# A selective scan in one Macaron block: two 512-column scans per state in place of four 256-column ones

## The chip, the core and the metric

The kernel runs on one core of a Trainium2 chip. Its time is the device time of one launch in microseconds (us). Three runs of the kernel before gave 807.47, 808.60 and 809.86 us, so the median is 808.6 us.

A core has engines that each work through their own list of instructions in order: PE (matrix products), DVE (elementwise and scans), ACT (functions of one input, with a scale and a bias), POOL (elementwise, and here also the issue of adding DMAs) and SP (plain DMAs). They meet at semaphores only. An instruction that waits holds up everything behind it on its engine.

## The reference

```python
def _L0_attn_ref(x, W_x, W_dt, b_dt, A_log, D_param):          # d_inner 512, 16 states
    xz = einsum('bld,kd->blk', x, W_x)                         # dt_raw (128), b (16), c (16)
    dt = softplus(einsum('blr,dr->bld', dt_raw, W_dt) + b_dt)
    a = -exp(A_log)
    d_a = exp(dt[..., None] * a)                               # the decays
    dbx = dt[..., None] * b[:, :, None, :] * x[..., None]
    def step(h, (da_t, dbx_t, c_t)):
        h = da_t * h + dbx_t                                   # the scan over 2048 tokens
        return h, einsum('bdn,bn->bd', h, c_t)
    return scan(step, 0, ...) + x * D_param

x = x + 0.5 * ffn(layernorm(x), w1, w2, w3)      # ffn: w3q @ (sigmoid(w1q @ x) * (w2q @ x))
x = x + attn(layernorm(x), ...)                  # 2048 tokens x 512 channels
x = x + 0.5 * ffn(layernorm(x), w1, w2, w3)      # the same weights, quantised to -1, 0, 1
```

## The kernel before, in words

Channels lie on the partitions: 512 channels are four k-tiles of 128 (KD = 4). Tokens lie along the free axis in eight chunks of 256 (TC = 256, NC = 8). The scan stage goes through the chunks in order, and in each through the 16 states; one state of one chunk is a slot, number g = 16c + n. For a slot:

- POOL makes `dbx` for all four k-tiles in one instruction (`times_b`, L1146), two slots ahead of DVE, into a ring of four buffers.
- ACT makes the decays, one `Exp` of 128x256 for each k-tile, into two PSUM banks: `decay0` holds k-tiles 0 and 1, `decay1` holds 2 and 3 (`decays`, L747). A bank is free when its two scans of the slot before are done.
- DVE scans (`scans`, L941): four `tensor_tensor_scan` of 128x256, k-tile by k-tile, each started from the state that the same n had at the end of the chunk before (`last_state`; in chunk 0 from zero, as an immediate). Then it multiplies the states by the row c (`times_c`, L952, 128x1024) and keeps the last column (`save_state`, L957).
- POOL issues an adding DMA for the product (`add_prod`, L1159), even and odd states into two sums, and once a chunk adds the two sums (`add_y`, L1164).

Between these go the two FFNs and three layernorms (0, 1, 2: ahead of the first FFN, of the scan and of the second FFN) of neighbouring chunks. An FFN of a chunk is 11 ups (16 matmuls each) and 4 downs (22 each) on PE; for each up ACT takes `tanh` (L702), DVE the product `hid` (L907), ACT and POOL split it into `hid_hi` (L710) and `hid_lo` (L1126). DVE adds the downs to the sum (`residual`, L914). A layernorm goes PE mean, DVE `centred` (L887), ACT `square` (L669), POOL fold (L301, L303), PE variance, ACT `std` (L687), DVE reciprocal (L891), PE spread, DVE normalise (L895; its output is `xln` for layernorm 1). Softplus (L735), `Sqrt` and the set with `Exp` and `Tanh` are different tables on ACT, so that a change between them is an ACT_TABLE_LOAD.

Where these pieces stand between the scans is fixed by four tables, AT_PE, AT_ACT, AT_DVE and AT_POOL. A number 10s + p means slot s of the chunk, place p: on DVE place 0 is ahead of the first pair of scans, 1 between the pairs, 2 behind the second pair, 3 behind `save_state`; on ACT place 0 is ahead of the decays of pair 0 for slot s + 1, 1 between them and those of pair 1, 2 behind them. Names with `_first` and `_last` hold for the first and the last chunk. PE's numbers set only the order of its own pieces.

## Time and profile before

| | us |
|---|---|
| median of three runs | 808.6 |
| profiled execution | 809.69 |
| its span, first to last instruction | 807.9 |
| scan stage, first to last scan | 88.1 to 756.3 |
| a chunk in the steady part, from chunk to chunk | 88.8 |

Only the span has a trace; 1.8 us lie around it. Busy time of an engine is the union of its instructions in the trace. Successive instructions of one engine overlap a little, so that the distance from start to start (called pitch here) is less than the duration of one. In a timeline row the first number is the start, the second how long the row lasts, and x4 says that four like instructions stand in it; what stands in brackets is the idle time ahead of it and what ended that.

### The profile page before, as it was taken

What the parts mean: (1) busy time and instruction counts of PE and PEld (TensorE: products, weight loads), DVE (VectorE), ACT (ScalarE), POOL (GpSimd) and SP (SyncE); (2) the same over time, 40 slices, a digit from 0 to 9 for tenths busy, and PEclk for the clock granted to TensorE, in tenths of its full rate; (3) what the DMA queues carried; (4) which work ended last, traced back from release to release, by engine and by line L of the source; (5) the groups of instructions that cost most, each with busy time, mean ns of one, the idle gap of its engine ahead of it and who ended that gap; (6) DMA issues with size and microseconds to landing.
All of it is one profiled execution on the core that took longest, in us unless ns stands there. A gap on an engine that the chain in (4) does not pass through costs nothing.

```text
span 807.9 us, 13722 instructions
## 1 busy us (share of the span) xinstructions
PE 638.8 (79%) x4826; PEld 520.5 (64%) x4826; DVE 669.8 (83%) x1076; ACT 510.2 (63%) x1105; POOL 637.9 (79%) x522
## 2 busy tenths in 40 slices
PE   4598884398879979898789887997989878267788
PEld 4486763177568866777578666876677757155677
DVE  3962699799968999699979996899969997999721
ACT  5663755867685767567785768576756776556231
POOL 0442799989988999889998998799988989789011
PEclk9998997689999999999999999999999999778879
DMA  9400578886866688395958586669839585986300
GB/s 357 155 2 1 153 161 184 195 190 137 186 158 143 145 191 201 79 232 122 214 113 202 138 187 157 148 140 203 190 79 233 121 191 124 217 177 124 69 1 27
DMA packets 42725, 122.10 MB, mean 151 GB/s; under 512 B 5920, under 2 KB 14880, under 8 KB 42656
## 3 DMA queue, kind: packets, MB, share of 16 engines
q0 software_dynamic: 19152, 69.74, 44.8%
q1 hardware_dynamic: 23504, 51.49, 20.4%
q8 instruction: 38, 0.62, 0.3%
q14 instruction: 31, 0.25, 0.1%
HBM read 47.03 MB, written 4.46 MB: 64 GB/s over the span
## 4 chain that ended last, share of the span: by engine, by line
DVE 35%; PE 27%; POOL 14%; issue 14%; ACT 8%; DMA 3%; DVEq 1%; POOLq 0%; ACTq 0%
DVE states L941 20%; PE work L406 17%; DVE shared L952 8%; PE stat L406 7%; POOL shared L1146 5%; POOL hid_lo L1126 4%; POOL shared L1159 3%; DMA shared<-shared 2%; PE decay L406 2%; ACT decay L747 2%; DVE centred L887 1%; DVE hid L907 1%; DVE q L985 1%; ACT q L765 1%; ACT L687 1%
## 5 line engine op out<-in xcount | busy, mean ns | idle before, releaser
L406 PE MATMUL work<-x_hi,q 128*128 128x256 f16 x1408 | 329.1, 282 | 37.6 <-DVE hid L907 17.5
L1146 POOL TENSOR_TENSOR shared<-u,b_row 128x1024 f32<-128x1024 f32 x127 | 335.7, 2648 | 0.1
L406 PE MATMUL work<-x_lo,q 128*128 128x256 f16 x1408 | 328.6, 282 | 0.0
L941 DVE TENSOR_TENSOR_SCAN states<-decay,last_state,shared 128x256 f32<-128x256 f32 x448 | 301.7, 737 | 3.9 <-issue 0.6
L747 ACT ACTIVATE decay<-dt,a_neg 128x256 f32<-128x256 f32 x512 | 220.6, 467 | 99.9 <-DVE states L941 98.6
L406 PEld LDWEIGHTS work<-x_hi,q 128*128 128x128 f16 x1408 | 143.0, 102 | 68.9 <-DVE hid L907 25.0
L1126 POOL TENSOR_TENSOR hid_lo<-hid,hid_hi 128x256 f16<-128x256 f32 x176 | 132.5, 964 | 63.7 <-ACT hid_hi L710 63.6
L406 PE MATMUL work<-hid_hi,q 128*128 128x256 f16 x693 | 154.0, 273 | 11.9 <-POOL hid_lo L1126 8.0
L952 DVE TENSOR_TENSOR shared<-states,c_row 128x1024 f32<-128x1024 f32 x128 | 155.9, 1218 | 8.9 <-issue 0.2
L406 PEld LDWEIGHTS work<-x_lo,q 128*128 128x128 f16 x1408 | 142.2, 101 | 21.3
L406 PE MATMUL work<-hid_lo,q 128*128 128x256 f16 x693 | 153.8, 272 | 0.0
L1159 POOL DMA_DIRECT2D shared<-shared x126 | 130.7, 1038 | 26.5 <-DVE shared L952 18.5
L702 ACT ACTIVATE tanh<-work 128x256 f32<-128x256 f32 x176 | 62.4, 373 | 75.5 <-PE work L406 70.6
L907 DVE SCALAR_TENSOR_TENSOR hid<-tanh,work 128x256 f32<-128x256 f32 x176 | 71.0, 410 | 46.1 <-ACT tanh L702 44.7
L406 PEld LDWEIGHTS work<-hid_hi,q 128*128 128x128 f16 x693 | 68.4, 99 | 27.7 <-issue 12.8
L710 ACT ACTIVATE hid_hi<-hid 128x256 f16<-128x256 f32 x176 | 67.9, 409 | 13.7 <-DVE hid L907 13.3
L406 PEld LDWEIGHTS work<-hid_lo,q 128*128 128x128 f16 x693 | 67.8, 98 | 7.6
L1120 POOL TENSOR_TENSOR x_lo<-centred,x_hi 128x1024 f16<-128x1024 f32 x15 | 35.9, 2391 | 35.8 <-ACT x_hi L695 35.8
L406 PE MATMUL stat<-shared,mean_w 128*128 128x256 f32 x136 | 36.2, 414 | 24.8 <-DVE shared L914 11.8
L406 PEld LDWEIGHTS stat<-shared,mean_w 128*128 128x128 f32 x136 | 26.7, 207 | 31.3 <-DVE shared L914 14.1
L941 DVE TENSOR_TENSOR_SCAN states<-decay,shared 128x256 f32<-128x256 f32 x64 | 39.3, 679 | 3.2 <-ACT decay L747 2.3
L301 POOL TENSOR_TENSOR square<-square 128x512 f32<-128x512 f32 x21 | 34.6, 1650 | 7.9 <-ACT square L669 7.9
(100 smaller groups left out, 599.0 us busy)
## 6 DMA issues: line engine op xcount, KB each, us to landing
shared<-shared POOLq DMA_DIRECT2D x133, 512.0 KB, 6.3
b_row<-bc_dram SPq DMA_DIRECT2D x32, 512.0 KB, 4.9
c_row<-bc_dram SPq DMA_DIRECT2D x32, 512.0 KB, 5.3
x_in<-xT SPq DMA_DIRECT2D x8, 512.0 KB, 9.8
outT<-shared SPq DMA_DIRECT2D x7, 512.0 KB, 3.2
shared<-w1T SPq DMA_DIRECT2D x4, 704.0 KB, 7.7
shared<-w2T SPq DMA_DIRECT2D x4, 704.0 KB, 12.0
shared<-w3T SPq DMA_DIRECT2D x3, 768.0 KB, 13.4
```

Of the source, the lines that this page charges most:

```text
L301: engine.tensor_tensor(dst[:, 0:2, :], src[:, 0:2, :], src[:, 2:4, :], ALU.add).then_inc(summed, 1)
L406: return nc.tensor.matmul(out, lhsT, rhs, start=start, stop=stop)
L702: nc.scalar.activation(tanh[:, h % 3, :], bank_of(which, h)[:, 0, :], ACT.Tanh, scale=0.5 / X_SCALE).then_inc(tanh_done, 1)
L710: nc.scalar.activation(hid_hi[:, h, :], hid[:, hid_slot(which, h), :], ACT.Copy).then_inc(hi_done, 1)
L747: ins = nc.scalar.activation(decay[pair][:, j, :], dt[:, par, k, :], ACT.Exp, scale=a_neg[:, k, n:n + 1])
L907: nc.vector.scalar_tensor_tensor(out=hid[:, hid_slot(which, h), :], in0=tanh[:, h % 3, :], scalar=1.0, in1=bank_of(which, h)[:, 1, :], op0 ...
L941: nc.vector.tensor_tensor_scan(out=states[:, k, :], data0=decay[pair][:, k % 2, :], data1=dbx[:, g % DBX_RING, k, :], initial=state, op0=A ...
L952: nc.vector.tensor_tensor(prod_of(c, n), states[:, :, :], bcast(c_row[:, group % 2, n % ROWS, :]), ALU.mult).then_inc(prod_done, 1)
L1120: nc.gpsimd.tensor_tensor(x_lo[:, which, :, :], centred[i][:, :, :], x_hi[:, which, :, :], ALU.subtract).then_inc(ln_lo[i], 1)
L1126: nc.gpsimd.tensor_tensor(hid_lo[:, h, :], hid[:, hid_slot(which, h), :], hid_hi[:, h, :], ALU.subtract).then_inc(lo_done, 1)
L1146: nc.gpsimd.tensor_tensor(dbx[:, g % DBX_RING, :, :], u[:, par, :, :], bcast(b_row[:, group % 2, n % ROWS, :]), ALU.mult).then_inc(dbx_don ...
L1159: nc.gpsimd.dma_start(total, prod_of(c, n), accum_op=ALU.add).then_inc(added(c, n)[0], 16)
```

## The change

Each pair of scans becomes one scan of 128x512 over both k-tiles of the pair. For that the decay of the pair's second k-tile is zero in its first column, which cuts the recurrence there. DVE zeroes that column of both banks once, ahead of the scan stage, and the `Exp` of the second k-tile then writes columns 1 to 255 only. The state that the second k-tile should have started from enters through the input: `dbx[:, k, 0] += first_decay * last_state`. ACT does this (`add_carry`), one `Identity` of 128x1 for each pair with the carried state as input, the first decay as a scale read from memory and the old `dbx` as a bias read from memory. The first decays of a chunk (16 states each) are two more `Exp` of 128x16 a chunk (`first_decays`). In chunk 0 there is no carry.

New waits: the scan of a pair waits for its carry; `add_carry` waits for the slot's `dbx`, for the saved state of the chunk before and for the first decays. All four tables have new numbers.

```diff
 AT_ACT  (of 20 rows)
-    hi2=[100, 110, 122, 131, 131, 140, 140, 141, 142, 150, 150],
+    hi2=[82, 112, 112, 112, 132, 132, 132, 141, 141, 150, 150],
 AT_POOL  (add_y, and lo1: hid_lo of the first FFN)
-    add_y=30, add_y_last=2, ... lo1=[41, 41, 42, 42, 42, 42, 42, 42, 42, 42, 42],
+    add_y=21, add_y_last=2, ... lo1=[31, 32, 32, 32, 32, 32, 32, 42, 42, 50, 50],
...
+        first_decay = sb("first_decay", [P, 2, 2, NS])
...
             def decays(c, n, par, pair):
...
-                    act.wait_ge(scan_done, KD * (g - 1) + 2 * pair + 2)
+                    act.wait_ge(scan_done, 2 * (g - 1) + pair + 1)
+                if g == 0:
+                    act.wait_ge(first_column_zeroed, pair + 1)
                 for j in range(2):
                     k = 2 * pair + j
-                    ins = nc.scalar.activation(decay[pair][:, j, :], dt[:, par, k, :], ACT.Exp,
+                    ins = nc.scalar.activation(decay[pair][:, j, j:TC], dt[:, par, k, j:TC], ACT.Exp,
                                                scale=a_neg[:, k, n:n + 1])
                 ins.then_inc(decay_done, 1)
+
+            def first_decays(c, par):
+
+                act.wait_ge(z_read, KD * (c + 1))
+                for j in range(2):
+                    nc.scalar.activation(first_decay[:, par, j, :], a_neg[:, 2 * j + 1, :], ACT.Exp,
+                                         scale=dt[:, par, 2 * j + 1, 0:1]).then_inc(first_decay_done, 1)
+
+            def add_carry(c, n, par):
+
+                g = NS * c + n
+                act.wait_ge(first_decay_done, 2 * c)
+                act.wait_ge(state_saved, g - NS + 1)
+                act.wait_ge(dbx_done, g + 1)
+                for j in range(2):
+                    k = 2 * j + 1
+                    column = dbx[:, g % DBX_RING, k, 0:1]
+                    nc.scalar.activation(column, last_state[:, n, k:k + 1], ACT.Identity,
+                                         scale=first_decay[:, par, j, n:n + 1], bias=column).then_inc(carry_added, 1)
...
             def scan_chunk(c, par):
                 for s in range(NS):
                     beside_scan(c, par, 10 * s)
+                    if s == NS - 1 and not last(c):
+                        first_decays(c + 1, 1 - par)
                     next_decays(c, s, par, 0)
+                    if s < NS - 1 and not first(c):
+                        add_carry(c, s + 1, par)
+                    elif s == NS - 1 and not last(c):
+                        add_carry(c + 1, 0, 1 - par)
                     beside_scan(c, par, 10 * s + 1)
                     next_decays(c, s, par, 1)
...
             def scans(c, n, pair):
...
-                for k in range(2 * pair, 2 * pair + 2):
-                    state = 0.0 if first(c) else last_state[:, n, k:k + 1]
-                    nc.vector.tensor_tensor_scan(out=states[:, k, :], data0=decay[pair][:, k % 2, :],
-                                                 data1=dbx[:, g % DBX_RING, k, :], initial=state,
-                                                 op0=ALU.mult, op1=ALU.add).then_inc(scan_done, 1)
+                if not first(c):
+                    dve.wait_ge(carry_added, 2 * (g - NS) + pair + 1)
+                two = slice(2 * pair, 2 * pair + 2)
+                nc.vector.tensor_tensor_scan(out=states[:, two, :].rearrange("p k t -> p (k t)"),
+                                             data0=decay[pair][:, :, :].rearrange("p k t -> p (k t)"),
+                                             data1=dbx[:, g % DBX_RING, two, :].rearrange("p k t -> p (k t)"),
+                                             initial=0.0 if first(c) else last_state[:, n, 2 * pair:2 * pair + 1],
+                                             op0=ALU.mult, op1=ALU.add).then_inc(scan_done, 1)
...
-            first_u_of(0)
-            first_u_of(1)
+            for pair in range(2):
+                dve.wait_ge(z_read, 2 * pair + 2)
+                nc.vector.memset(decay[pair][:, 1, 0:1], 0.0).then_inc(first_column_zeroed, 1)
+                first_u_of(pair)
```

The other waits on `scan_done` count two scans a slot in place of four.

What the change moves is seen best in the engines' lists. The first place is ACT in a chunk of the steady part, from layernorm 0's `square0` to its `std0`, which stands behind the decays of pair 0 for slot 15. Before:

```order
L669 ACTIVATE square0<-centred0 128x1024
L702 ACTIVATE tanh<-work1 128x256
L710 ACTIVATE hid_hi<-hid 128x256
L747 ACTIVATE decay0<-dt,a_neg 128x256 x2
L710 ACTIVATE hid_hi<-hid 128x256 x2
L747 ACTIVATE decay1<-dt,a_neg 128x256 x2
L702 ACTIVATE tanh<-work2 128x256
L702 ACTIVATE tanh<-work0 128x256
L710 ACTIVATE hid_hi<-hid 128x256 x2
L747 ACTIVATE decay0<-dt,a_neg 128x256 x2
L687 ACT_TABLE_LOAD
L687 ACTIVATE std0<-stat,zero_eps 128x2
```

Now, with the list entered one `square0` and two `tanh` later, since it is longer (`128x1` rows are the carries):

```order
L752 ACTIVATE decay0<-dt,a_neg 128x256
L752 ACTIVATE decay0<-dt,a_neg 128x255
L772 ACTIVATE shared<-last_state,shared,first_decay 128x1 x2
L752 ACTIVATE decay1<-dt,a_neg 128x256
L752 ACTIVATE decay1<-dt,a_neg 128x255
L713 ACTIVATE hid_hi<-hid 128x256 x3
L705 ACTIVATE tanh<-work0 128x256
L752 ACTIVATE decay0<-dt,a_neg 128x256
L752 ACTIVATE decay0<-dt,a_neg 128x255
L772 ACTIVATE shared<-last_state,shared,first_decay 128x1 x2
L690 ACT_TABLE_LOAD
L690 ACTIVATE std0<-stat,zero_eps 128x2
```

The list of ACT from the table load behind the softplus to `std0` held 5 tanh, 5 `hid_hi`, 10 decays and a square before; it now holds 5 tanh, 3 `hid_hi`, 10 decays, the square and 6 carries.

The second place is DVE in the same part of a chunk's life, from `centred1` to `xln` (layernorm 1, slots 8 and 9). Before:

```order
L887 TENSOR_TENSOR centred1<-shared,stat 128x1024
L941 SCALAR_TENSOR_TENSOR states<-decay0,last_state,shared 128x256 x2
L941 SCALAR_TENSOR_TENSOR states<-decay1,last_state,shared 128x256 x2
L952 TENSOR_TENSOR shared<-states,c_row 128x1024
L957 COPY last_state<-states 128x4
L907 SCALAR_TENSOR_TENSOR hid<-tanh,work1 128x256
L941 SCALAR_TENSOR_TENSOR states<-decay0,last_state,shared 128x256 x2
L941 SCALAR_TENSOR_TENSOR states<-decay1,last_state,shared 128x256 x2
L891 RECIPROCAL rstd1<-std1 128x2
L952 TENSOR_TENSOR shared<-states,c_row 128x1024
L957 COPY last_state<-states 128x4
L895 TENSOR_TENSOR xln<-centred1,stat 128x1024
```

Now:

```order
L972 SCALAR_TENSOR_TENSOR states<-decay0,last_state,shared 128x512
L917 TENSOR_TENSOR centred1<-shared,stat 128x1024
L972 SCALAR_TENSOR_TENSOR states<-decay1,last_state,shared 128x512
L985 TENSOR_TENSOR shared<-states,c_row 128x1024
L990 COPY last_state<-states 128x4
L937 SCALAR_TENSOR_TENSOR hid<-tanh,work1 128x256
L972 SCALAR_TENSOR_TENSOR states<-decay0,last_state,shared 128x512
L972 SCALAR_TENSOR_TENSOR states<-decay1,last_state,shared 128x512
L921 RECIPROCAL rstd1<-std1 128x2
L985 TENSOR_TENSOR shared<-states,c_row 128x1024
L990 COPY last_state<-states 128x4
L925 TENSOR_TENSOR xln<-centred1,stat 128x1024
```

`centred1` stood ahead of both pairs of slot 8 and now stands between them, so that one pair fewer lies between it and `rstd1`. `xln` is behind slot 9 as it was.

The third place is ACT at the end of chunk 0, from `std0` to the first decays of chunk 1. Before:

```order
L687 ACTIVATE std0<-stat,zero_eps 128x2
L747 ACT_TABLE_LOAD
L747 ACTIVATE decay0<-dt,a_neg 128x256 x2
L747 ACTIVATE decay1<-dt,a_neg 128x256 x2
L695 ACTIVATE x_hi<-centred0 128x1024
L747 ACTIVATE decay0<-dt,a_neg 128x256 x2
```

Now:

```order
L690 ACTIVATE std0<-stat,zero_eps 128x2
L698 ACTIVATE x_hi<-centred0 128x1024
L760 ACT_TABLE_LOAD
L760 ACTIVATE first_decay<-a_neg,dt 128x16 x2
L752 ACTIVATE decay0<-dt,a_neg 128x256
L752 ACTIVATE decay0<-dt,a_neg 128x255
L772 ACTIVATE shared<-last_state,shared,first_decay 128x1 x2
```

Here `x_hi`, a table load, the two first decays and a carry stand ahead of the first scan of chunk 1, and the decays of slot 15 have moved ahead of `std0`. On DVE in chunk 0, `xln` moves from slot 10 to slot 11, and the normalise of layernorm 0 from behind slot 14 to between the pairs of slot 15.

## Rows read from the trace of the kernel before

**Rows 1.** The page: busy us, share of the span, instructions; and the chain that ended last.

```profile
span 807.9 us, 13722 instructions
...
PE 638.8 (79%) x4826; PEld 520.5 (64%) x4826; DVE 669.8 (83%) x1076; ACT 510.2 (63%) x1105; POOL 637.9 (79%) x522
...
DVE 35%; PE 27%; POOL 14%; issue 14%; ACT 8%; DMA 3%; DVEq 1%; POOLq 0%; ACTq 0%
```

**Rows 2.** Windows: stretch, us, busy of PE, PEld, DVE, ACT, POOL, PEclk, DMA share, GB/s.

```profile
475.70:514.50 38.80, 33.76 (x242) 26.52 (x243) 30.42 (x52) 26.98 (x60) 34.80 (x30) 0.91 0.61 133
514.50:564.40 49.90, 42.23 (x355) 35.39 (x352) 48.28 (x82) 33.67 (x74) 45.72 (x38) 1.00 0.81 184
686.00:758.00 72.00, 40.73 (x283) 31.90 (x281) 69.17 (x97) 37.99 (x87) 54.74 (x42) 0.79 0.76 160
```

**Rows 3.** Groups by line and shape: busy us, mean ns of one, idle before.

```profile
L941 DVE TENSOR_TENSOR_SCAN states<-decay,last_state,shared 128x256 f32<-128x256 f32 x448 | 301.7, 737 | 3.9 <-issue 0.6
...
L710 ACT ACTIVATE hid_hi<-hid 128x256 f16<-128x256 f32 x176 | 67.9, 409 | 13.7 <-DVE hid L907 13.3
...
L941 DVE TENSOR_TENSOR_SCAN states<-decay,shared 128x256 f32<-128x256 f32 x64 | 39.3, 679 | 3.2 <-ACT decay L747 2.3
...
L729 ACT ACTIVATE shared<-xln,dpar 128x256 f32<-128x256 f32 x32 | 13.5, 493 | 0.0
```

**Rows 4.** Timeline of DVE in a steady chunk: slots 3, 5, 6 and 7.

```profile
533.10 0.42 DVE L907 SCALAR_TENSOR_TENSOR hid<-tanh,work 128x256 f32<-128x256 f32 x1 [0.88 <-POOL hid_lo L1126]
...
543.29 0.15 DVE L957 COPY last_state<-states 128x4 f32<-128x4 f32 x1
543.57 2.68 DVE L941 TENSOR_TENSOR_SCAN states<-decay,last_state,shared 128x256 f32<-128x256 f32 x4
546.16 0.15 DVE L891 RECIPROCAL rstd<-std 128x2 f32<-128x2 f32 x1
...
549.13 1.39 DVE L941 TENSOR_TENSOR_SCAN states<-decay,last_state,shared 128x256 f32<-128x256 f32 x2
```

**Rows 5.** What DVE waited for in the chunk from 466.1 to 554.9 us.

```profile
DVE hid L907 <- ACT tanh L702: 3.8, 2, 2.7
DVE shared L914 <- PE work L406: 2.1, 1, 2.1
DVE centred L887 <- PE stat L406: 0.9, 1, 0.9
DVE rstd L891 <- ACT std L687: 0.9, 1, 0.9
DVE hid L907 <- POOL hid_lo L1126: 0.9, 1, 0.9
```

**Rows 6.** Timeline of ACT: `std0` of a steady chunk.

```profile
499.39 0.26 ACT L687 ACTIVATE std<-stat,zero_eps 128x2 f32<-128x2 f32 x1
```

**Rows 7.** Timeline of DVE: layernorm 0's reciprocal, and the chunk's last residual.

```profile
499.69 0.17 DVE L891 RECIPROCAL rstd<-std 128x2 f32<-128x2 f32 x1 [0.90 <-ACT std L687]
...
513.88 0.69 DVE L914 SCALAR_TENSOR_TENSOR shared<-work,shared 128x512 f32<-128x512 f32 x1 [2.06 <-PE work L406]
```

**Rows 8.** Timeline of POOL: `add_y`, `dbx` of slot 7, fold of layernorm 1.

```profile
525.87 0.86 POOL L1164 DMA_DIRECT2D shared<-shared  x1 [1.49 <-DVE states L941]
...
542.62 2.35 POOL L1146 TENSOR_TENSOR shared<-u,b_row 128x1024 f32<-128x1024 f32 x1
...
556.34 2.50 POOL L301 TENSOR_TENSOR square<-square 128x512 f32<-128x512 f32 x1
```

**Rows 9.** Timeline of DVE in chunk 0: `xln` and `centred0`.

```profile
133.52 1.22 DVE L895 TENSOR_TENSOR xln<-centred,stat 128x1024 f32<-128x1024 f32 x1
...
148.89 1.22 DVE L887 TENSOR_TENSOR centred<-x_in,stat 128x1024 f32<-128x1024 f32 x1 [2.91 <-PE stat L406]
```

**Rows 10.** Timeline of DVE: the last residual, behind the last scan.

```profile
756.17 0.67 DVE L914 SCALAR_TENSOR_TENSOR shared<-work,shared 128x512 f32<-128x512 f32 x1
```

**Rows 11.** Timeline of PE: the last matmul of the last chunk's downs.

```profile
755.24 0.27 PE L406 MATMUL work<-hid_lo,q 128*128 128x256 f16 x1
```

More of the change, by code:

```diff
@@ new lines @@
+    down2_last=[153, 153, 153, 153], mean0=152, mean0_first=153, mean1=142, mean1_first=153, mean2=132,
+    mean2_last=153, spread0=153, spread0_first=153, spread1=150, spread1_first=153, spread2=141,
+    spread2_last=153, up1=[32, 102, 110, 110, 110, 110, 112, 112, 112, 122, 123],
+    up1_first=[21, 52, 52, 82, 83, 100, 120, 121, 121, 121, 132],
+    up2=[142, 142, 143, 150, 151, 151, 152, 152, 152, 152, 153],
+    up2_last=[153, 153, 153, 153, 153, 153, 153, 153, 153, 153, 153], var0=153, var0_first=153, var1=143,
@@ new lines @@
+    var1_first=153, var2=133, var2_last=153, xz=151, xz_first=153, z0=151, z0_first=153, z1=152, z1_first=153)
+AT_ACT = dict(
+    bc_read=102, bc_read_first=112, d_xln=152, d_xln_first=111, dt_raw=102, dt_raw_first=112,
+    gate1=[0, 2, 20, 20, 21, 22, 22, 31, 40, 41, 42], gate1_first=[0, 0, 2, 12, 22, 22, 40, 40, 42, 50, 60],
+    gate2=[81, 92, 110, 110, 120, 121, 130, 130, 140, 141, 142],
+    gate2_last=[61, 70, 72, 80, 80, 90, 91, 101, 111, 111, 120], hi1=[2, 21, 21, 30, 30, 30, 32, 40, 42, 42, 42],
+    hi1_first=[12, 12, 12, 31, 40, 41, 42, 42, 51, 60, 60],
+    hi2=[82, 112, 112, 112, 132, 132, 132, 141, 141, 150, 150],
+    hi2_last=[82, 82, 82, 82, 92, 101, 110, 112, 112, 112, 121], square0=122, square0_first=131, square1=81,
+    square1_first=82, square2=50, square2_last=22, std0=141, std0_first=150, std1=90, std1_first=101, std2=61,
+    std2_last=32, x_hi0=151, x_hi0_first=150, x_hi2=71, x_hi2_last=42, z_read=[112, 112, 120, 120],
+    z_read_first=[122, 122, 122, 122])
@@ new lines @@
+AT_POOL = dict(
+    add_y=21, add_y_last=2, fold_sq0=140, fold_sq0_first=131, fold_sq1=90, fold_sq1_first=82, fold_sq2=51,
+    fold_sq2_last=32, fold_x0=101, fold_x0_first=121, lo1=[31, 32, 32, 32, 32, 32, 32, 42, 42, 50, 50],
+    lo1_first=[11, 21, 41, 41, 42, 50, 50, 50, 50, 50, 50],
+    lo2=[91, 132, 140, 140, 141, 141, 141, 142, 142, 150, 150],
+    lo2_last=[100, 100, 101, 102, 111, 111, 112, 121, 121, 122, 130], u=131, u_first=131, x_lo0=151,
+    x_lo0_first=151, x_lo2=72, x_lo2_last=51)
```

44 lines of the change are left out of this document (12 added, 32 removed).

## The prediction, made before the changed kernel was run

> **What bounds the kernel now.** I read the page first: DVE is busy for 83% of the span, PE and POOL for 79% each, ACT for 63%, and the chain that ended last is split over DVE, PE and POOL [rows 1]. No one engine bounds the whole, so a chunk has to be cut into stretches. The windows show two in a steady chunk [rows 2]. From 514.5 us (first scan) to 564.4 (end of `xln`) DVE is busy for 48.3 of 49.9 us: DVE bounds it, with one wait of 0.9 for a `hid_lo` [rows 4, 5]. From 475.7 (end of `xln`) to 514.5 (end of the last residual) DVE is busy for 30.4 of 38.8 us. There it waits 3.8 for `tanh`, 2.1 for the downs of PE, 0.9 for a mean and 0.9 for `std` [rows 5]: a chain over ACT and PE bounds it, and DVE has room. The two add up to 88.7 us, the period of a chunk. The last chunk is DVE's nearly throughout, 69.2 of 72 us [rows 2].
>
> **The scans.** Four scans take from 543.57 to 546.16, so one has a pitch of 0.648 us [rows 4]. With an immediate initial state (chunk 0) a scan lasts 679 ns against 737 [rows 3], so its pitch is about 0.59. No row has a scan of 512. A product of 1024 columns lasts 1.22 us and an elementwise operation of 512 lasts 0.67 [rows 9, 10], 0.55 for 512 more columns, so 1.07 ns a column and some 0.12 fixed. If the fixed part is the same in a scan, 679 ns is 0.12 and 256 columns of 2.15 ns. The next 256 columns then cost 0.53 to 0.55, and a scan of 512 has a pitch of 0.648 + 0.53 = 1.18. In a steady chunk a pair goes from 1.30 to 1.18, hence 0.11 to 0.12; I take 0.11, or 0.22 a slot. In chunk 0 I take 0.06 a pair, since the operand that is spared is an immediate there. Over 112 slots this is 25 us of DVE and in chunk 0 another 1.9, 27 in all. The other end is a scan of 512 that costs just twice one of 256, which gives 0; a cost above twice has no reason, since only columns are added.
>
> A rule of the Trainium skill prices the same thing. "Vector Engine (DVE) Microarchitecture Reference", section 5.2, gives some 75 ns for each instruction beyond 1.04 ns a column, and "DVE: opcode table, instruction layouts, handler registers and perf-mode slots" says of feedback that the scan runs at half throughput. By these a pair saves 0.075 us and the whole 256 x 0.075 = 19 us, an estimate, where the rows say 27. The rows show the half rate (2.15 against 1.07 ns) but a larger fixed part for a scan whose initial state is read from memory.
>
> **The carries.** ACT gets 224 `Identity` of 128x1 and 14 `Exp` of 128x16. The nearest rows have other widths: `hid_hi`, 256 columns with immediates, lasts 409 ns, and the product with a scale from memory 493 [rows 3], so a pointer costs 84. `std0` of two columns with one pointer lasts 0.26 [rows 6]. A carry has one more pointer, 0.26 + 0.08 = 0.34 to 0.365. Neighbours on ACT overlap by about 0.1, so I take a pitch of 0.27; the ends are 0.19 (the second one hidden mostly) and 0.365 (no overlap, since the bias is what POOL wrote and the output goes to the same place). At 0.27 this is 224 x 0.27 = 60 us more on an engine with 298 us free [rows 1], 8.6 a chunk. In the DVE-bound run ACT is busy for 33.7 of 49.9 us and takes 10 x 0.54 = 5.4 more: this cover holds. It doesn't hold where ACT's list stands on the chain.
>
> "ScalarE: Activation LUTs" of the Trainium skill, What ACT_TABLE_LOAD costs, gives 186 ns and 93 for each pointer operand, with 93 of overlap: 0.37 alone and 0.28 in a row. The trace agrees on the pointer (84), and the sum would move by 2 us of ACT's time.
>
> **A steady chunk, part by part.**
> - DVE run, ten slots from the first scan to `xln` (slot 0 to 9, as before): 10 x 0.22 = -2.2.
> - The wait of 0.9 for `hid_lo` at 533.10 [rows 4]: the first FFN's `hid_lo` stand a slot or so earlier on POOL; I take half, -0.45 (0 to -0.9).
> - Layernorm 1: `centred1` now stands between the pairs of slot 8, so one pair less (1.2 us) lies between it and `rstd1`. ACT's square, POOL's fold (2.5 us at 556.34 [rows 8]), PE and `std` have to fit into what is left. I take +0.4 for a new wait (0 to +1.0).
> - At two places a scan follows the copy directly where a `hid` stood. The copy at 543.29 is followed by a scan at 543.57, 0.28, where the next copies hand on in less [rows 4]: +0.15.
> - The stretch behind `xln`: the gain of its six slots, 1.3 us, goes into the waits, since what follows waits for ACT and PE. The chain is `std0`, `rstd0` at 499.69, spread, ten ups and the downs on PE, residual at 513.88 [rows 7], 14.2 us that stay. What moves is `std0` at 499.39 [rows 6]: ahead of it stand six carries more and two `hid_hi` less, 6 x 0.27 - 2 x 0.31 = +1.0 (0.5 to 1.6 by the ends of the carry).
>
> The sum is -2.2 - 0.45 + 0.4 + 0.15 + 1.0 = -1.1 a chunk, and for six steady chunks -6.6.
>
> **Chunk 0.** `xln` moves a slot on, to slot 11, and the chain behind it (134.7 to `centred0` at 148.89, where DVE waited 2.9 [rows 9]) moves with it. The slots gain 16 x 0.12 = 1.9. The normalise of layernorm 0 is now two instructions behind its reciprocal, so DVE sees PE's round trip: +0.9, the wait that `rstd0` has in a steady chunk [rows 5]. In front of chunk 1's first scan stand `x_hi`, a table load, two first decays and a carry: I take +1.5. With 0.3 more at `centred0` the sum is +1.0 (-1 to +3).
>
> **The last chunk.** 16 x 0.22 = 3.5 at most. But the last downs ended at 755.24 + 0.27, 0.7 before the residual at 756.17 that reads them [rows 10, 11], with PE's granted clock at 0.79 [rows 2]. DVE can gain only what PE gives as well: -3.0.
>
> **POOL and its DMAs.** POOL's work stays, but `add_carry` needs `dbx` about a slot before the scan did. POOL is busy for 80.5 of 88.7 us [rows 2]. The tightest place is slot 7: `dbx` ends at 544.97 [rows 8] and its scan starts at 549.13 [rows 4], 4.1 us or less than one slot (5.6 from slot 6 to slot 7). With the new table POOL's `hid_lo` stand ahead of it differently; I take 0, with up to +0.5 a chunk. `add_y`, one slot earlier, waited 1.5 us at 525.87 [rows 8]; it stays at that.
>
> **Sum.** -6.6 + 1.0 - 3.0 = -8.6 us. The profiled execution took 809.7 (span 807.9 and 1.8 around it), 1.1 over the median, so it gives 801.1, and against the median of 808.6 it is 800.0.
>
> **Rivals.**
> 1. The whole gain of DVE comes through: -27, or 782. For it: DVE is the busiest engine [rows 1], and the new tables might shift waits out of the stretch behind `xln`. Against it: DVE waits 7.7 us in that stretch for PE and ACT, which gain nothing, and PE's 14.2 us from `rstd0` to the residual hold. Half of it would be 794.
> 2. ACT becomes the bound, and the kernel is slower. Place: ACT's list between the softplus and `std0`, and the decays of pair 1, which stand behind the carry. Price: with 0.365 for each carry `std0` is 1.6 us late, and if each scan waits for its carry 0.1 a pair more, the run of ten slots loses 2.0 and the six slots are covered. A chunk then is -2.2 + 2.0 - 0.45 + 0.4 + 0.15 + 1.6 = +1.5, six are +9; with chunk 0 (+1) and the last (-0.3) this is +9.7, or 818. It decides from a carry of some 0.45 with the decays behind it, or from 0.1 of wait at each scan. For it: a decay of pair 0 can start only when the scans of the slot before leave the bank, so that ACT's decays come just ahead of their scans. Against it: ACT is idle for 16 of 49.9 us there [rows 2].
> 3. POOL: the carry waits for `dbx`, and with it all of ACT, at slots 6 to 8 and behind `add_y`, in each chunk 1.4 us. This eats the gain: 808.
> 4. A scan of 512 costs twice one of 256. Then the change gives DVE nothing: the steady chunk is -0.45 + 0.4 + 0.15 + 1.0 = +1.1, six +6.6, chunk 0 +2.9, last 0: +9.5, or 818.
>
> **How the numbers follow.** The forecast has 0.64, with its own range from 794 to 805 (unknown costs: the carry 0.5 to 1.6 a chunk, layernorm 1 0 to 1.0, chunk 0 -1 to 3); rival 1 has 0.12, rival 2 0.09, rival 3 0.10, rival 4 0.05. What a measurement can tell from no change is 0.3%, 2.4 us: faster is below 806.2, slower above 811. Faster: 0.62 + 0.12 = 0.74. Within: 0.02 of the forecast and 0.09 of rival 3, 0.11. Slower: rivals 2 and 4 and 0.01 of rival 3, 0.15. The range goes from 786 (over half of rival 1 is inside) to 812 (all but the upper end of rival 3 is), which leaves out some 2 in 10.
>
> **What would show it.** The scans: a mean of some 1.27 us and a pitch of 1.18 for 512 columns, and DVE busy for about 645 us. The carries: about 0.36 in duration, pitch 0.27, and ACT busy for about 575. `xln` to `rstd0`: a us longer than the 24.0 before; `rstd0` to the last residual unchanged at 14.2. The run of a chunk's first scan to `xln`: 47.8 in place of 49.9. If DVE's waits for the carry add up to more than 5 us, rival 2 or 3 is at work, and the releaser of the carry (`dbx`, or ACT's own list) tells which. The forecast is wrong if the period of a steady chunk is outside 86.5 to 88.4, or if `std0` comes no later.

## The result, and the profile after

The changed kernel takes 815.98 us (median of four runs, 815.17 to 816.72) against 808.78 for the kernel before: 1.009 times, with an interval of 1.007 to 1.011. It is slower by 7.2 us where 8.6 us less was forecast. The later experiments were each timed against the kernel before on one chip; its medians there went from 807.6 to 809.4, so that two experiments of different groups can be compared to 1 or 2 us. Two executions stood far from the others of their kernel and are left out of the medians here: one of 1314.7 us with the old tables and no carries, and the profiled one of the last experiment (876.3 us, granted clock 0.736), from whose trace only distances on DVE are read.

The page of the changed kernel answers to [rows 1]:

```profile
span 813.4 us, 13931 instructions
...
PE 647.0 (80%) x4826; PEld 527.3 (65%) x4826; DVE 646.0 (79%) x822; ACT 567.3 (70%) x1343; POOL 637.4 (78%) x522
...
PE 27%; ACT 20%; DVE 17%; POOL 17%; issue 11%; DMA 7%; DVEq 0%; ACTq 0%; POOLq 0%
```

DVE is busy for 23.8 us less, ACT for 57.1 more. In the chain that ended last DVE's share fell from 35% to 17%, and ACT's rose from 8% to 20%. The groups by line and shape (busy us, mean ns, idle before) answer to [rows 3]:

```profile
L972 DVE TENSOR_TENSOR_SCAN states<-decay,last_state,shared 128x512 f32<-128x512 f32 x224 | 280.6, 1278 | 12.2 <-ACT shared L772 5.1 <-DVE last_state L990 4.6 <-DVE shared L985 1.8
L972 DVE TENSOR_TENSOR_SCAN states<-decay,shared 128x512 f32<-128x512 f32 x32 | 37.9, 1219 | 4.1 <-ACT decay L752 3.2
...
L772 ACT ACTIVATE shared<-last_state,shared,first_decay 128x1 f32<-128x1 f32 x224 | 73.0, 373 | 0.0
```

The prices of the operations were nearly right: a scan of 512 lasts 1.28 us (forecast 1.27), a carry 0.373 (forecast 0.34 to 0.365), and a pair of carries takes 0.56 from start to start. New is the idle time of 12.2 us in front of the scans, 3.9 before.

The same three windows as [rows 2] (from `xln` to the last residual, from there to the next `xln`, and the last chunk; stretch, us, busy of PE, PEld, DVE, ACT, POOL, PEclk, DMA, GB/s):

```profile
480.20:519.80 39.60, 33.81 (x250) 27.13 (x249) 29.23 (x41) 30.53 (x74) 35.32 (x31) 0.91 0.57 128
519.80:569.60 49.80, 43.20 (x351) 35.94 (x349) 46.51 (x62) 38.30 (x94) 45.31 (x37) 0.97 0.84 187
692.00:764.00 72.00, 41.63 (x281) 32.27 (x280) 66.34 (x66) 45.14 (x117) 54.52 (x42) 0.76 0.76 165
```

In the second stretch DVE has 1.8 us less to do, and the stretch is 0.1 shorter. The first is 0.8 longer. In the last chunk DVE has 2.8 less to do in 72 us. Before `xln` at the end of the second stretch DVE waits, and the timelines of DVE and PE (start, duration, in brackets the idle time and what ended it) show for what:

```profile
564.89 0.15 DVE L921 RECIPROCAL rstd<-std 128x2 f32<-128x2 f32 x1
...
568.44 1.22 DVE L925 TENSOR_TENSOR xln<-centred,stat 128x1024 f32<-128x1024 f32 x1 [2.04 <-PE stat L409]
```

```profile
563.92 0.61 PE L409 MATMUL stat<-mean_w,square 128*128 128x1 f32 x4 [1.56 <-POOL square L306]
...
564.85 0.42 PE L409 MATMUL work<-x_lo,q 128*128 128x256 f16 x1
565.06 0.42 PE L409 MATMUL work<-x_hi,q 128*128 128x256 f16 x1
...
567.62 0.78 PE L409 MATMUL stat<-ident,rstd 128*128 128x128 f32 x4
```

Between the variance and the spread of layernorm 1 stands an up of 16 matmuls on PE, and they come every 0.21 us: the granted clock was 0.51 of 2.4 GHz in 564.5 to 567.8, so 1.2 GHz. Before, an up stood there too, at full clock, and `rstd` at 561.82 was followed by `xln` at 563.25 without a wait. But the low clock itself isn't new. Before, it came just behind `xln`, at the projections, in four of the six steady chunks. Windows of the kernel before (columns as above):

```profile
560.30:562.00 1.70, 1.70 (x17) 1.34 (x14) 1.66 (x4) 1.63 (x3) 1.70 (x2) 1.00 1.15 314
...
566.40:568.40 2.00, 2.00 (x6) 0.85 (x5) 1.87 (x5) 1.15 (x3) 2.00 (x2) 0.50 1.05 201
```

In the changed kernel it came ahead of the spread in five of the six steady chunks. In the sixth, chunk 1, the granted clock was 1.00 from 208.0 to 212.5, `xln` at 212.95 had no wait, and the chunk took 87.0 us where it had taken 88.7.

`std0`, a chunk's part later (ACT, then PE, then DVE):

```profile
590.35 0.87 ACT L752 ACTIVATE decay<-dt,a_neg 128x256 f32<-128x256 f32 x2
591.15 0.66 ACT L772 ACTIVATE shared<-last_state,shared,first_decay 128x1 f32<-128x1 f32 x2
591.83 1.28 ACT L690 ACT_TABLE_LOAD   x1
593.12 0.26 ACT L690 ACTIVATE std<-stat,zero_eps 128x2 f32<-128x2 f32 x1
```

```profile
593.63 1.22 PE L409 MATMUL stat<-ident,rstd 128*128 128x128 f32 x4 [3.53 <-DVE rstd L921]
594.65 0.42 PE L409 MATMUL work<-x_hi,q 128*128 128x256 f16 x1
594.86 0.42 PE L409 MATMUL work<-x_lo,q 128*128 128x256 f16 x1
```

```profile
593.41 0.17 DVE L921 RECIPROCAL rstd<-std 128x2 f32<-128x2 f32 x1 [1.67 <-ACT std L690]
...
598.78 0.42 DVE L937 SCALAR_TENSOR_TENSOR hid<-tanh,work 128x256 f32<-128x256 f32 x1 [3.25 <-ACT tanh L705]
```

PE's variance for `std0` was done at 590.1, and ACT came to it at 593.1, because its list was full to that point. PE stood for 3.5 us (3.1 before), and the ups behind the spread began at 1.2 GHz. They did so before as well, in four of the five periods from `xln` to `xln`, but not for as long. Three windows of 2 us behind the spread, before (spread at 499.90) and in the changed kernel (at 504.26):

```profile
499.90:501.90 2.00, 2.00 (x12) 1.58 (x13) 0.74 (x2) 1.99 (x4) 1.83 (x4) 0.67 1.07 205
501.90:503.90 2.00, 2.00 (x11) 1.40 (x10) 0.00 (x0) 0.85 (x3) 1.17 (x2) 0.50 0.11 18
503.90:505.90 2.00, 2.00 (x20) 1.75 (x18) 1.43 (x2) 1.10 (x3) 1.08 (x2) 0.98 0.00 0
```

```profile
504.30:506.30 2.00, 2.00 (x9) 1.67 (x10) 1.85 (x4) 1.99 (x5) 1.48 (x3) 0.50 0.16 31
506.30:508.30 2.00, 2.00 (x12) 1.40 (x10) 0.00 (x0) 0.77 (x3) 1.08 (x2) 0.50 1.04 197
508.30:510.30 2.00, 2.00 (x13) 1.47 (x12) 0.90 (x2) 1.13 (x4) 0.55 (x1) 0.59 0.23 43
```

Where the 7.2 us are (profiled executions, by the start of each chunk's first product): before the first product -1.2; chunk 0 75.8 to 79.4, +3.6; chunks 1 to 6 522.9 to 526.1, +3.2; from the last chunk's first product to the end 118.1 in both. The sum is, to 0.1, the 5.5 us by which the spans differ; the other 1.7 are the scatter between single runs. The 88.8 us that stand ahead of the prediction for a chunk are those of one chunk; from `xln` to `xln`, five periods took 87.8 us in the mean.

### The profile page after: what moved, and what is told of

Read it like the earlier page. It is cut to its first block, busy times and chain, and to the rows that moved or that the text cites. A ratio compares the mean times of both kernels' runs of the same rounds, so it can differ in the third digit from the quotient of the medians.

```text
span 813.4 us, 13931 instructions
## 1 busy us (share of the span) xinstructions
PE 647.0 (80%) x4826; PEld 527.3 (65%) x4826; DVE 646.0 (79%) x822; ACT 567.3 (70%) x1343; POOL 637.4 (78%) x522
## 4 chain that ended last, share of the span: by engine, by line
PE 27%; ACT 20%; DVE 17%; POOL 17%; issue 11%; DMA 7%; DVEq 0%; ACTq 0%; POOLq 0%
PE work L409 19%; DVE states L972 9%; POOL shared L1181 8%; DMA shared<-shared 7%; PE stat L409 6%; ACT decay L752 6%; POOL hid_lo L1161 4%; DVE shared L985 4%; POOL shared L1194 3%; ACT shared L772 2%; PE decay L409 2%; ACT L690 2%; ACT tanh L705 1%; ACT hid_hi L713 1%; POOL square L304 1%
## 5 line engine op out<-in xcount | busy, mean ns | idle before, releaser
L409 PE MATMUL work<-x_hi,q 128*128 128x256 f16 x1408 | 340.2, 288 | 38.1 <-DVE hid L937 18.5
L1181 POOL TENSOR_TENSOR shared<-u,b_row 128x1024 f32<-128x1024 f32 x127 | 342.5, 2699 | 0.0
L409 PE MATMUL work<-x_lo,q 128*128 128x256 f16 x1408 | 339.8, 288 | 0.0
L972 DVE TENSOR_TENSOR_SCAN states<-decay,last_state,shared 128x512 f32<-128x512 f32 x224 | 280.6, 1278 | 12.2 <-ACT shared L772 5.1
L752 ACT ACTIVATE decay<-dt,a_neg 128x256 f32<-128x256 f32 (+1 forms) x512 | 220.4, 464 | 75.8 <-DVE states L972 75.4
L409 PE MATMUL work<-hid_hi,q 128*128 128x256 f16 x693 | 158.1, 277 | 8.5 <-POOL hid_lo L1161 5.2
L409 PEld LDWEIGHTS work<-x_lo,q 128*128 128x128 f16 x1408 | 145.1, 103 | 24.1
L409 PE MATMUL work<-hid_lo,q 128*128 128x256 f16 x693 | 157.6, 276 | 0.0
L1194 POOL DMA_DIRECT2D shared<-shared x126 | 133.6, 1061 | 27.5 <-DVE shared L985 14.6
L713 ACT ACTIVATE hid_hi<-hid 128x256 f16<-128x256 f32 x176 | 66.1, 410 | 15.3 <-DVE hid L937 15.1
L772 ACT ACTIVATE shared<-last_state,shared,first_decay 128x1 f32<-128x1 f32 x224 | 73.0, 373 | 0.0
L409 PE MATMUL stat<-mean_w,square 128*128 128x1 f32 x96 | 16.4, 279 | 37.2 <-POOL square L306 33.4
## 6 DMA issues: line engine op xcount, KB each, us to landing
shared<-w2T SPq DMA_DIRECT2D x4, 704.0 KB, 11.7
```

What stands on the lines that cost most here:

```text
L409: return nc.tensor.matmul(out, lhsT, rhs, start=start, stop=stop)
L713: nc.scalar.activation(hid_hi[:, h, :], hid[:, hid_slot(which, h), :], ACT.Copy).then_inc(hi_done, 1)
L752: ins = nc.scalar.activation(decay[pair][:, j, j:TC], dt[:, par, k, j:TC], ACT.Exp, scale=a_neg[:, k, n:n + 1])
L772: nc.scalar.activation(column, last_state[:, n, k:k + 1], ACT.Identity, scale=first_decay[:, par, j, n:n + 1], bias=column).then_inc(carry ...
L972: nc.vector.tensor_tensor_scan(out=states[:, two, :].rearrange("p k t -> p (k t)"), data0=decay[pair][:, :, :].rearrange("p k t -> p (k t) ...
L1181: nc.gpsimd.tensor_tensor(dbx[:, g % DBX_RING, :, :], u[:, par, :, :], bcast(b_row[:, group % 2, n % ROWS, :]), ALU.mult).then_inc(dbx_don ...
```

## The experiments

**Tables against scans.** Four cells: old or new tables, four scans or two with carries.

```diff
- the four tables with the new numbers
+ the four tables of the kernel before        (e1, on the changed kernel)
```

> Scans of 512 and carries as in the changed kernel, but the four tables of the kernel before. Theory A (the loss lies in where the new tables put the pieces: an up on PE between var1 and spread1 that delays xln by 2.0 us a chunk, later ends of chunk 0, add_y and mean2 early in the last chunk): DVE keeps most of its gain in the run of ten slots, so 798 to 806. Theory B (the loss lies in the carries themselves, 60 us more on ACT that delay decays and std0): the tables matter little, so 812 to 820.

Measured: 805.96 us, ratio to before 0.9968 (0.9948 to 0.9987).

```diff
- the four tables of the kernel before
+ the new ones                                (e2, on the kernel before)
```

> The kernel before (four scans of 256, no carries) with the new tables. Theory A: it has the bad places too and none of the scans' gain: 812 to 825, with a wait of DVE for the spread ahead of xln (smaller than 2.0 us, since four scans leave more time behind centred1). Theory B: 806 to 810, like the kernel before.

Measured: 812.04 us, 1.0048 (1.0031 to 1.0065). So the tables cost four scans 3.5 us and two scans 10. The scans and carries, with the old tables, bring 2.6 us. The loss is neither the scans' nor the tables' alone: 6.3 us come only where both meet (7.2 - 3.5 + 2.6). Theory A had this right in sign. Its remedy, to take the up out from between variance and spread, is tried in the next run:

```diff
-    spread1=150,        (AT_PE)
+    spread1=143,
```

> The changed kernel with one number changed: spread1 on PE 143 in place of 150, so that the spread stands right behind var1 and the up that stood between them comes behind it. Theory A: DVE's waits for the spread ahead of xln (8.8 us in five chunks) go, and up to that much time: 807 to 811. Theory B: no change, 815 to 817.

Measured: 817.96 us, 1.0117 (1.0093 to 1.0141). The wait ahead of `xln` went (no row of it is left among DVE's waits) and came back one step later: `xln` to `centred0` took 16.6 us in place of 13.9, since the up, 1.8 to 3.4 us long, now stood ahead of the projections. To move the up only moves the time that it takes.

**The carries.** They were left out:

```diff
-                        add_carry(c, s + 1, par)
...
-                    dve.wait_ge(carry_added, 2 * (g - NS) + pair + 1)
```

> The changed kernel without its carries: add_carry is left out, and with it the scans' wait for it, so that the second k-tile of a pair starts each chunk from zero (part of the computation is left out). Theory B: the 60 us of ACT and the waits for the carry are the loss: 800 or less (16 us faster than the changed kernel). Theory A: the wait of 2.0 us ahead of xln stays, only std0 (1 us a chunk) and the 5 us of waits for carries go: 806 to 812.

Measured: 798.81 us, 0.9869 (0.9842 to 0.9897), 17.2 less than with carries. Then they were made, but of no consequence:

```diff
-                act.wait_ge(dbx_done, g + 1)
-                    column = dbx[:, g % DBX_RING, k, 0:1]
+                    column = idle_carry[:, 2 * g + j:2 * g + j + 1]
-                                         scale=first_decay[:, par, j, n:n + 1], bias=column).then_inc(carry_added, 1)
+                                         scale=first_decay[:, par, j, n:n + 1], bias=zero_eps[:, 0:1]).then_inc(carry_added, 1)
...
-                    dve.wait_ge(carry_added, 2 * (g - NS) + pair + 1)
```

> The changed kernel in which ACT does its 224 carries in the same places, but writes them to columns of their own and reads no dbx; neither the carry waits for dbx nor the scan for the carry (the carried state of the second k-tiles doesn't reach the scans: part of the computation is left out). Leaving the carries out altogether gave 798.8. If the 17 us are the carries' time in ACT's list (theory: occupancy), this gives 812 to 816. If they are the new waits, dbx to ACT and ACT to DVE (theory: waits), it gives 798 to 803.

Measured: 813.37 us, 1.0073 (1.0049 to 1.0097). 14.6 of the 17.2 us are the time that the carries take in ACT's list; the rest, 2.6 us by the medians and 1.4 by the ratios, are the waits for `dbx` and for the carry. This decides between occupancy and waits. With the old tables:

```diff
- the changed kernel's tables
+ the old tables, no carries
```

> Old tables, scans of 512 and no carries (left out as in the second k-tiles starting each chunk from zero). With carries 806.0. If ACT's occupancy ahead of std0 costs in both orders: 792 to 799. If the carries only hurt where the new tables had filled ACT's list: 803 to 806.

Measured: 803.07 us, 0.9929 (0.9908 to 0.995), only 2.9 less than with carries (805.96). The same 60 us of ACT cost 17.2 with one order and 2.9 with the other. In the old order they too moved `rstd0` (centred0 to `rstd0` 10.0 us without, 11.7 with), but without carries DVE then waited for `tanh` and for the downs as long as with them (24.6 and 18.0 us in chunks 1 to 6 against 23.7 and 15.0 with them).

**Where they stand, and where `std0` stands.**

```diff
+                    if s < NS - 1 and not first(c):
+                        add_carry(c, s + 1, par)
                     next_decays(c, s, par, 0)
-                    if s < NS - 1 and not first(c):
-                        add_carry(c, s + 1, par)
```

> The changed kernel with the two carries of a slot ahead of the decays of pair 0 in ACT's list instead of behind them. Occupancy: they then lie in the time in which ACT waits for the scan to free the bank, in the DVE-bound part, but the number of carries ahead of std0 is the same, so a part of the loss stays: 809 to 815. Waits: the carry needs dbx still earlier, so slower than the changed kernel: 816 to 822.

Measured: 808.76 us, 1.0010 (0.9994 to 1.0026), 7 less than the changed kernel. The gain isn't at `std0`: the time from `centred0` to `rstd0` stayed at 11.1 us in the mean of five periods. It lies in the run from the residual to `xln`, 47.4 in place of 48.9, where DVE waited for the spread 2.5 us in all instead of 8.8. With the old tables:

```diff
- tables and place of the carries as in the changed kernel
+ the old tables, carries ahead of the decays of pair 0
```

> Old tables, scans of 512, and the carries ahead of the decays of pair 0. Old tables with the carries behind them gave 806.0. Occupancy: 802 to 806. Waits: 806 to 812.

Measured: 806.07 us, 0.9979 (0.9961 to 0.9997), the same as with the carries behind (805.96). Then one number:

```diff
-    std0=141,        (AT_ACT)
+    std0=132,
```

> The changed kernel with std0 on ACT at 132 in place of 141 and nothing else, the carries behind the decays of pair 0 as they were. Carries first alone gave 808.8, both gave 799.7, neither 816.0. If the two are separate effects that add up: 806 to 808. If the number ahead of std0 is nearly all: 800 to 803. If the carries' place is what counts: 813 or more.

Measured: 798.84 us, 0.989 (0.9858 to 0.9923). A single number takes 17 us off, as much as the carries had cost, though with the carries still in. With the carries first as well:

```diff
+    std0=132, add_carry ahead of next_decays(c, s, par, 0)
```

> The changed kernel with the carries ahead of the decays of pair 0 (808.8) and one number more: std0 on ACT at 132 in place of 141, ahead of three hid_hi, a tanh, two decays and a carry. In the changed kernel var0 was done at 590.1 us and std0 came at 593.1, so ACT's list held it back by 3 us, and DVE waited 1.7 for it. Occupancy of ACT ahead of std0 as the cause: 1.2 to 1.7 us a chunk for five chunks, 800 to 803. If the decays of slot 15, now behind two table loads, become the wait: 807 or more.

Measured: 799.68 us, 0.9879 (0.986 to 0.9899). So the two don't add up. What the carries' place had gained, the wait for the spread, is gone already with `std0` at 132 (0.7 us in chunks 1 to 6).

The timeline of ACT and PE in the kernel with `std0` at 132:

```profile
571.31 0.87 ACT L752 ACTIVATE decay<-dt,a_neg 128x256 f32<-128x256 f32 x2
572.11 0.66 ACT L772 ACTIVATE shared<-last_state,shared,first_decay 128x1 f32<-128x1 f32 x2
572.67 0.86 ACT L752 ACTIVATE decay<-dt,a_neg 128x256 f32<-128x256 f32 x2
573.55 1.28 ACT L690 ACT_TABLE_LOAD   x1
574.84 0.26 ACT L690 ACTIVATE std<-stat,zero_eps 128x2 f32<-128x2 f32 x1
```

```profile
549.89 0.61 PE L409 MATMUL stat<-mean_w,square 128*128 128x1 f32 x4 [1.55 <-POOL square L306]
...
550.57 0.27 PE L409 MATMUL work<-x_hi,q 128*128 128x256 f16 x1
550.68 0.27 PE L409 MATMUL work<-x_lo,q 128*128 128x256 f16 x1
...
552.10 0.61 PE L409 MATMUL stat<-ident,rstd 128*128 128x128 f32 x4
```

`square0` to `std0` takes 5.0 us (569.84 to 574.84) in place of 7.6 (585.54 to 593.12), and DVE waits 0.2 us for `std` in chunks 1 to 6 where it waited 9.1. And the up between variance and spread now comes at 0.11 us a matmul: the clock stayed at 2.4 GHz in this place (granted 1.00 from 549.0 to 552.5), with the same idle time of PE ahead of the variance (1.55 and 1.56). The table has the mean over the five periods from `xln` to `xln`, each step from start to start:

| us | before | changed | no carries | `std0` at 132 |
|---|---|---|---|---|
| `xln` to `centred0` | 14.79 | 13.95 | 13.75 | 13.94 |
| `centred0` to `rstd0` | 10.27 | 11.09 | 10.01 | 9.33 |
| `rstd0` to last residual | 13.96 | 14.95 | 14.16 | 14.50 |
| residual to next `xln` | 48.78 | 48.89 | 47.55 | 47.36 |
| period | 87.80 | 88.88 | 85.47 | 85.14 |

`rstd0` itself is worth 1.8 of the 3.7 us that `std0` at 132 takes off. 0.5 come behind it and 1.5 come 50 us later, as the up at full clock. The carries cost in the same three places. Why the clock held ahead of the spread can't be read from the idle time just ahead of the variance and stays open; that it held in one and fell in the other is shown.

**Chunk 0 and the last chunk.**

```diff
- new numbers of all names with _first, carries first, std0=132
+ old numbers of these names
```

> As the run before, and with the old numbers for chunk 0 (all names with _first in the four tables). Chunk 0 took 79.4 us with the new numbers with and without carries, and 75.6 with the old ones and the carries first. If it is the new order of chunk 0: 3.6 us less than the run before, 797 to 800. Otherwise equal.

Measured: 796.37 us, 0.9854 (0.9831 to 0.9877), 3.3 less by the medians and 2.0 by the ratios, whose intervals overlap.

```diff
- new numbers of all names with _last (on the kernel just told)
+ old numbers of these names
```

> The kernel of 796.4 with the old numbers for the last chunk (all names with _last). In the changed kernel the last chunk lost 1.6 us for mean2 and gained nothing (118.1 us from its first product to the end in both); with the old tables it was 117.0. So 795 to 796.5; if the old numbers don't fit the chunk before: 797 to 799.

Measured: 796.92 us, 0.9866 (0.9839 to 0.9893): no difference in the total that can be told from scatter. In the trace the end did get shorter, 115.9 us from the last chunk's first product to the end against 119.1, while chunk 0, whose numbers are the same, took 77.5 against 75.5. And with the carries where the changed kernel has them:

```diff
-    std0=141, new numbers of the names with _first
+    std0=132, old numbers of the names with _first
```

> The changed kernel with std0 on ACT at 132 and the old numbers for chunk 0; the carries behind the decays of pair 0, as in the changed kernel. std0 alone gave 798.8, and the old chunk 0 took 3.3 us off where it was tried: 794 to 797, the fastest so far. If the two don't add up: 798 to 800.

Measured: 796.43 us, 0.9859 (0.9841 to 0.9877).

**What the scans bring in that order.**

```diff
- two scans of 512, carries
+ four scans of 256, no carries, tables of the kernel of 796.4 us
```

> Four scans of 256 and no carries, as before, with the tables that gave 796.4 with two scans and the carries first. If the two scans bring DVE's part of a chunk (10 slots of 0.15 to 0.2, less what is hidden) and the carries cost little now: 802 to 807, that is 6 to 10 above 796.4. If the 796.4 come from the tables alone: 793 to 798.

Measured: 803.44 us, 0.9947 (0.9928 to 0.9966).

```diff
- add_carry and its wait, with the tables of the kernel of 796.4 us
```

> Two scans of 512, the tables that gave 796.4, and no carries (the second k-tiles start each chunk from zero). If the carries are hidden in that order: 794 to 797. If ACT's occupancy still costs there: 785 to 792.

Measured: 788.01 us, 0.9761 (0.9733 to 0.9789). So in a good order the two scans alone bring 15.4 us (803.4 to 788.0), the carries take 8.4 back, and the edit as a whole is worth 7.0.

**Other hands for the carry, and one wait less.** POOL:

```diff
+                nc.gpsimd.tensor_tensor(carry[:, n % 2, :, 0], last_state[:, n, 1::2], first_decay[:, par, :, n], ALU.mult)
...
+                nc.gpsimd.tensor_tensor(dbx[:, g % DBX_RING, 1::2, 0:1], dbx[:, g % DBX_RING, 1::2, 0:1], carry[:, n % 2, :, :],
+                                        ALU.add)
-  add_carry on ACT, and first_decays a slot earlier
```

> Old tables and scans of 512, but the carry is made by POOL: a product of 128x2 and a sum of 128x2 a slot, one ahead of times_b and one behind it, for the slot before the one that times_b makes; ACT keeps only the first decays. Occupancy of ACT: its 60 us go, POOL gets 224 small operations of an estimated 0.15 to 0.3 us, 34 to 67 us, or 5 to 10 a chunk where it has 8 free. With 0.15 the kernel takes 797 to 802, with 0.3 POOL becomes the bound: 808 to 820.

Measured: 820.24 us, 1.0157 (1.0128 to 1.0185). The two operations lasted 633 and 458 ns in the mean, not 150 to 300, and DVE waited 12.5 us for them. DVE:

```diff
+                nc.vector.tensor_tensor(column, column, carry[:, n, :, :], ALU.add)     (column: 128x2 of dbx)
-  add_carry on ACT, and first_decays a slot earlier
```

> New tables and scans of 512; the carry is made by DVE: once a chunk a product of 128x30 and one of 128x2, and between the pairs of a slot a sum of 128x2 into dbx for the next slot; ACT keeps the first decays. Without any carry 798.8. A small DVE operation has a pitch of 0.06 to 0.2 us: with 0.1 the ten slots of the DVE-bound run lose 1.0 a chunk, so 801 to 806. With 0.2 or with waits for dbx: 808 to 815.

Measured: 977.26 us, 1.2071 (1.2048 to 1.2094). A sum of 128x2 lasted 1595 ns in the mean. The reason stands in the timelines of DVE and of POOL:

```profile
503.43 0.15 DVE L977 TENSOR_TENSOR shared<-shared,carry 128x2 f32<-128x2 f32 x1
...
514.53 2.60 DVE L977 TENSOR_TENSOR shared<-shared,carry 128x2 f32<-128x2 f32 x1
521.52 2.81 DVE L977 TENSOR_TENSOR shared<-shared,carry 128x2 f32<-128x2 f32 x1
```

```profile
500.51 2.96 POOL L1190 TENSOR_TENSOR shared<-u,b_row 128x1024 f32<-128x1024 f32 x1
...
513.80 2.68 POOL L1190 TENSOR_TENSOR shared<-u,b_row 128x1024 f32<-128x1024 f32 x1
516.11 0.99 POOL L1170 TENSOR_TENSOR hid_lo<-hid,hid_hi 128x256 f16<-128x256 f32 x1
520.24 0.87 POOL L1203 DMA_DIRECT2D shared<-shared  x1 [3.13 <-DVE shared L986]
520.84 3.45 POOL L1170 TENSOR_TENSOR hid_lo<-hid,hid_hi 128x256 f16<-128x256 f32 x5
```

The first sum starts as POOL's product ends (503.47) and lasts 0.15, as do all 21 of the 112 beside which POOL runs for no more than 0.06 us. The other 91 last 1.9 us in the mean and 4.6 at most. The second ends at 517.13 and POOL's operations at 517.10; the third at 524.33 and POOL's at 524.29. Both operands of this sum lie in SBUF, where the products and scans of the steady part, without this one, have one in PSUM. The Trainium skill has this rule in "SBUF — State Buffer", SBUF: two separate sides: a DVE operation with two SBUF inputs and a GpSimd operation that reads SBUF exclude each other for a whole instruction. The trace agrees. So the engines of this kernel don't meet at semaphores only.

Last, a redundant wait:

```diff
-                dve.wait_ge(first_dbx if g == 0 and pair == 0 else dbx_done, g + 1)
+                if first(c):
+                    dve.wait_ge(first_dbx if g == 0 and pair == 0 else dbx_done, g + 1)
```

> The same, and a scan behind chunk 0 no longer waits for dbx itself, since the carry that it waits for was made behind that dbx. In the last chunk of the changed kernel a slot took 4.02 us, where 3.95 stand without a wait for the carry. If each further wait of a scan costs DVE 0.07 us a slot: up to 0.7 us a chunk less, 790 to 793. If the price is not the number of waits: 794 to 797.

Measured: 792.72 us, 0.983 (0.9801 to 0.986). That is less than its base by 3.7 us by the medians and 2.3 by the ratios, but the two intervals overlap, so the total is not settled. Where a scan follows the product or the copy that it waits for, the median distances are these (us):

| | copy to scan | product to scan |
|---|---|---|
| before | 0.28 | 1.36 |
| changed | 0.35 | 1.43 |
| no carries | 0.28 | 1.36 |
| one wait less | 0.24 | 1.32 |

The wait for the carry costs DVE 0.07 us on such a scan; that the wait left out gives 0.04 back rests on one trace. The slot of the last chunk, free of other work, shows what is left of the gain (timeline of DVE, changed kernel; before, at 747.67 to 751.85, it was 2.82 from the scans to the product and 4.18 in all):

```profile
750.30 2.47 DVE L972 TENSOR_TENSOR_SCAN states<-decay,last_state,shared 128x512 f32<-128x512 f32 x2 [0.20 <-DVE shared L985]
752.90 1.22 DVE L985 TENSOR_TENSOR shared<-states,c_row 128x1024 f32<-128x1024 f32 x1
754.32 2.47 DVE L972 TENSOR_TENSOR_SCAN states<-decay,last_state,shared 128x512 f32<-128x512 f32 x2 [0.20 <-DVE shared L985]
```

2.60 to the product, which is the forecast 0.2 less, but 4.02 in all, 0.16 less.

## Why the prediction was wrong

- **The scans.** Right: pitch 1.19 (forecast 1.18), 0.21 us a slot from the scans to the product. (From 679 ns, 0.12 off leaves 2.18 ns a column, not 2.15, which is the missing hundredth.) DVE's busy time fell by 23.8 us, where the rows gave 27 and the Trainium skill's pages 19. What was missed is the carry's wait, 0.07 us wherever a scan directly follows a copy or product.
- **The carries' price.** Right: pitch 0.28, ACT 57 us more.
- **A steady chunk, -1.1.** It came to +0.5 over chunks 1 to 6 (3.2 / 6), and to +1.1 over the five periods of the table. The forecast had two parts, -2.1 for the run from the residual to `xln` and +1.0 for the stretch behind `xln`. The second came as forecast, the first came to +0.1.
- **Layernorm 1, "+0.4 (0 to +1.0)".** This is the step that failed. DVE waited 8.8 us for the spread in five chunks, 1.75 a chunk and up to 2.0, outside the range given. The term counted the pair of scans (1.2 us) that no longer covers the chain over ACT, POOL and PE, and gave PE's up between variance and spread no price of its own. At 1.2 GHz that up is 1.5 us longer. In chunk 1 and with `std0` at 132, where the clock held, the wait was 0 and 0.14 a chunk. The rest of the 2.2 us that are missing in this run are smaller: DVE's work fell by 1.9 and not 2.2, the wait for `hid_lo` had 0.2 to give and not 0.45, and small gaps, at the scans behind copies above all, grew by 0.4 and not 0.15.
- **"What moves is `std0`: +1.0", and "14.2 us that stay".** The sum is right, by luck. `centred0` to `rstd0` grew by 0.8. But `xln` to `centred0` shrank by as much, since the low clock no longer fell on the projections (before, 14.9 to 15.0 us with it and 14.1 without), so that `xln` to `rstd0` took 25.0 us as before (25.1) and the sign that was named, a us more, didn't come. The 14.2 us didn't stay: they were 14.8 to 15.1, against 14.2 to 14.3 in four of five periods before and 12.8 in the one where the clock held (15.0 and 14.0 in the mean). The low clock behind the spread lasted longer, as the windows show. I had taken PE's time as fixed in both places, though the traces have it at either clock. What sets the clock is not shown: the old tables with carries had PE idle for 2.4 us ahead of this spread in one chunk, with the ups behind it slow, and for 3.0 in another, with the ups at full clock.
- **Chunk 0, +1.0.** Mis-sized: +3.6 (and its terms add up to +0.8, not +1.0). The waits that were named came (1.3 for the normalise, 1.6 for the carry of chunk 1's first slot), and beside them DVE waited 0.9 more for decays and 1.1 more for `tanh`, in the new order of chunk 0, which costs four scans as much (79.8 us).
- **The last chunk, -3.0.** It gave 0.0: 1.2 us less to the last scan and 1.1 more behind it. DVE waited 1.6 us for the mean of layernorm 2, which the new number had put a place earlier on DVE while PE's mean began where it had (5.8 us behind the first product before, 5.9 now), and each slot lost 0.06 to 0.07 at the carry's wait. With the old numbers of this chunk the wait for the mean is gone from the trace and the end is 3.2 us shorter, but the total shows no gain. What makes up the 1.1 us behind the last scan was not settled.
- **Its signs.** The period of a steady chunk, 88.9 us, lies outside 86.5 to 88.4, as the prediction said it would if it was wrong. DVE's waits for the carry add up to 5.1 us, just over the 5 that were to point to rival 2 or 3. But without those waits the kernel gained only 1.4 to 2.6 us, and `centred0` to `rstd0` still took 11.1: DVE then waited 9.9 us for `std0` in five chunks where it had waited 8.4.
- **Rival 2** had the place (ACT's list between softplus and `std0`) and nearly the number (818), but it was priced for slow carries and waits at each scan. The carries cost nearly what was forecast. It took no slower carry, only two stretches of PE at 1.2 GHz that fell where DVE waits for them.

Of the 14.2 us by which the spans of the stages miss the forecast, 9.8 lie in the six steady chunks, 3.0 in the last, 2.6 in chunk 0, and -1.2 ahead of the scan stage. The forecast of -8.6 us is near the -7.0 that the edit is worth in an order that suits it. This is agreement in size at most: -8.6 was a forecast for the edit and its new tables together, against the kernel before. What wasn't asked is whether the order that came with the edit suits it.

## What to carry to other kernels

Work added to an engine that is idle for a third of the time is free only where its list has a gap: look for the one instruction on it that starts a chain on another engine, and count what stands ahead of it. When such an instruction (here `std0`, 7.6 us behind `square0` with its input ready for 3.0) can be moved, try this before the added work is judged: one number was worth 17 us here, the carries themselves 8. A stretch of PE that another engine waits for is to be priced at both clocks, and looked for in every chunk of the trace before: here one period in five, at full clock, was 2 to 3 us shorter than the others.
